# A fused cross attention, differential attention and feed-forward kernel: more of the transposed context from memory for tiles 5 and 6, tile 6's residual kept on chip, W2's scans in the output projection

## The reference

```python
# cross attention, x1 = layernorm(x)
energy = einsum('bcn,bmn->bcm', x1, ctx)          # 64 x 1601 for each batch
attn = softmax(energy, axis=-1)
attn = attn / (1e-9 + attn.sum(axis=1, keepdims=True))
x_r = einsum('bcm,bmn->bcn', attn, ctx)
t = x1 - (einsum('oc,bcn->bon', conv_w, x_r) + conv_b)
t_bn = (t - mean) * rsqrt(var + eps) * gamma + beta   # mean and var over all batches
x = x + x1 + relu(t_bn)
...
# feed-forward: the threshold of W1 and of W2 is 0.05 * max(abs(W))
```

## Time and profile before

| what | value |
|---|---|
| median of three runs | 1365.68 us |
| profiled execution | 1365.15 us |
| its span on the core | 1363.3 us |
| TensorE busy | 1321.5 us, 97% |
| VectorE busy | 867.5 us, 64% |
| ScalarE busy | 486.5 us, 36% |
| moved by DMA | 363.05 MB, mean 266 GB/s |

### The profile page before, as it was taken

How to read it: one execution, slowest core, us unless ns; L and a number is a source line. 1 busy time by engine, 2 the same in 40 slices (tenths; PEclk the granted TensorE clock), 3 DMA queues, 4 the chain that set the end, 5 groups by cost and what they waited for, 6 DMA issues and landing times.

```text
span 1363.3 us, 17544 instructions
## 1 busy us (share of the span) xinstructions
PE 1321.5 (97%) x6738; PEld 642.8 (47%) x6738; DVE 867.5 (64%) x1470; ACT 486.5 (36%) x751; POOL 2.4 (0%) x10
## 2 busy tenths in 40 slices
PE   6999999999999889999999999999999999999995
PEld 4554646444353344444555555445444444444442
DVE  2332424224231379868899986876999997777974
ACT  1111302112020022127777784112555455444432
POOL 0000000000000000000000000000000000000000
PEclk9999999999999989999999999999999999999997
DMA  9999999999999989916656669452477775222264
GB/s 380 419 420 420 420 421 421 422 420 420 406 406 420 412 330 331 325 30 186 173 149 182 170 200 329 148 211 87 168 259 239 231 263 190 77 77 74 78 182 154
DMA packets 142210, 363.05 MB, mean 266 GB/s; under 512 B 63152, under 2 KB 89904, under 8 KB 115760
## 3 DMA queue, kind: packets, MB, share of 16 engines
q1 hardware_dynamic: 138960, 350.39, 70.2%
q10 hardware_dynamic: 3168, 11.54, 2.1%
HBM read 315.22 MB, written 46.66 MB: 265 GB/s over the span
## 4 chain that ended last, share of the span: by engine, by line
PE 79%; issue 14%; DMA 4%; DVE 2%; ACT 0%; DVEq 0%; POOLq 0%; POOL 0%; ACTq 0%
PE ps L1249 14%; PE ps L1133 12%; PE ps L1405 9%; PE ps L1203 8%; PE ps L1316 8%; PE ps L1023 7%; PE ps L1365 6%; PE ps L1061 4%; PE ps L1043 2%; DMA ctxT<-in_ctxT 2%; PE ps L1115 2%; PE ps L1040 1%; PE ps L1269 1%; DMA xo<-in_x 1%; DMA x_t<-in_x 1%
## 5 line engine op out<-in xcount | busy, mean ns | idle before, releaser
L1454 PE MATMUL ps<-t_half,hl 128*128 128x512 f16 x896 | 193.5, 379 | 0.0
L1133 PE MATMUL ps<-ctx_sb,attnT 128*64 128x512 f32 (+1 forms) x832 | 180.3, 593 | 0.0
L757 ACT ACTIVATE stg<-ps 128x512 f32<-128x512 f32 (+1 forms) x66 | 36.3, 552 | 297.5 <-PE ps L1043 169.1
L1454 PEld LDWEIGHTS ps<-t_half,hl 128*128 128x128 f16 x896 | 87.7, 98 | 105.7
L1023 PE MATMUL ps<-ctxT,x1T 128*64 128x512 f32 x512 | 114.9, 596 | 0.4 <-DMA ctxT<-in_ctxT 0.4
L933 ACT ACTIVATE hl<-hb,al 128x512 f16<-128x512 f32 x112 | 79.2, 720 | 97.5 <-PE ps L1454 83.7
L1133 PEld LDWEIGHTS ps<-ctx_sb,attnT 128*64 128x64 f32 (+1 forms) x832 | 59.0, 137 | 115.3 <-issue 107.9
L1972 DVE SCALAR_TENSOR_TENSOR hl<-hb,al,hl 128x512 f16<-128x512 f32 x112 | 81.9, 749 | 48.7 <-ACT hl L933 48.5
L1203 PE MATMUL ps<-wv_sb,x2T 128*128 128x512 f32 x256 | 112.2, 596 | 0.0
L1316 PE MATMUL ps<-wo_sb,oT 128*128 128x512 f32 x256 | 111.6, 593 | 0.3 <-ACT oT L839 0.3
L1527 DVE SCALAR_TENSOR_TENSOR x1s<-ps,sw,x1s 128x512 f32<-128x512 f32 x16 | 12.0, 749 | 133.1 <-PE ps L1133 133.1
(11 more groups left out here) (227 smaller groups left out, 1803.7 us busy)
## 6 DMA issues: line engine op xcount, KB each, us to landing
ctxT<-in_ctxT SPq DMA_DIRECT2D x64, 1024.0 KB, 21.9
ctx_sb<-in_ctx SPq DMA_DIRECT2D x40, 1024.0 KB, 20.1
ctx_sb<-in_ctx SPq DMA_DIRECT2D x8, 4096.0 KB, 27.6
ctx_sb<-in_ctx SPq DMA_DIRECT2D x16, 2048.0 KB, 31.6
w_scan<-in_w1t SPq DMA_DIRECT2D x32, 512.0 KB, 6.3
w_buf<-in_w1t SPq DMA_DIRECT2D x32, 512.0 KB, 3.9
w_scan<-in_w2t SPq DMA_DIRECT2D x32, 512.0 KB, 5.0
w_buf<-in_w2t SPq DMA_DIRECT2D x32, 512.0 KB, 4.7
```

What stands on the lines that cost most here:

```text
L1133: ins = mm(bank(ea + hf)[C * b:C * b + C, :], attnT[0:w, slots[mt], C * b:C * b + C], ctx_sb[0:w, mt, b, hf * BANK:hf * BANK + BANK], star ...
L1454: ins = mm(bank(b), hl[:, r % RING, n, s * P:s * P + P], t_half[:, r % BRING, :], start=(fresh and k == 0 and n == 0), stop=(k == HK - 1 a ...
```

## The change

1. `LOADED` becomes (0, 0, 0, 0, 0, 4, 8, 8): tile 5 has four of its eight chunks of blocks 8 to 11 from memory, tile 6 all eight. Tile 6 then has only the two halves of block 12 left to transpose (`pairs(6)` is of length 2), so the work that was tied to the third and fifth last pair is tied to the first (`max(len - 3, 0)` and `max(len - 5, 0)`).
2. The load of blocks 0 to 3 is split in two halves (group 5, `part`), and the order of SyncE's loads for tiles 5 and 6 is written out.
3. The t of tile 6 is not stored and loaded back: `relu` reads it, as that of tile 7, from `x1s`. `tok` of tiles 2 to 5 is loaded in place of 2 to 6.
4. 32 scans (all of W1) are done beside V, and the 32 of W2 after the last head: 4, then 5 in each tile of the output projection until none is left (28 of them, in six tiles).

```diff
@@ -56,7 +56,7 @@
 U = len(UNITS)
 
 SINGLES = [(mt, half) for mt in range(TM, MT) for half in range(2)]
-LOADED = (0,) * (NT - 2) + (4, NC)
+LOADED = (0,) * (NT - 3) + (4, 8, NC)
 
 
 def pairs(p):
@@ -73,7 +73,7 @@
 
 def slots_of_tile(p):
 
-    ring = [(p, "chunk", c) for c in range(NC)] + [(p, "wide", i) for i in range(min(LOADED[p] // 2, 2))]
+    ring = [(p, "chunk", c) for c in range(NC)] + [(p, "wide", i) for i in range(LOADED[p] // 2 if p < NT - 1 else 2)]
     return ring if p < NT - 1 else ring + [(p, "apart", i) for i in range(2)]
 
 
@@ -88,8 +88,8 @@
 HC = HID // P
 WT = HID * N // P // 1024
 WH = WT // H
-SCANS_V = 40
-V_SCANS = (0, 0, 2, 6, 7, 7, 7, 7, 4)
+SCANS_V = 32
+V_SCANS = (0, 0, 1, 5, 6, 6, 7, 7, 0)
 EPS = 1e-5
 LAMBDA_INIT = 0.8 - 0.6 * math.exp(-0.3 * 12)
 X_SCALE = 512.0
@@ -459,8 +459,14 @@
                 for i in range(2):
                     sp.dma_start(tails[i][:, :, :, :], ctxE_in[i]).then_inc(apart_got, 16)
 
-            def load_N(q, g):
+            def load_N(q, g, part=None):
                 m0, m1 = N_GROUPS[g][0], N_GROUPS[g][-1] + 1
+                if g == 5 and part is None:
+                    load_N(q, g, 0)
+                    load_N(q, g, 1)
+                    return
+                if g == 5:
+                    m0, m1 = 2 * part, 2 * part + 2
                 sp.dma_start(ctx_sb[:, m0:m1, :, :], ctx[q, m0 * P:m1 * P].rearrange("(t p) b n -> p t b n", p=P))\
                   .then_inc(ctx_in[g], 16)
 
@@ -480,10 +486,10 @@
             load_T(1, range(4, 6))
             for p in range(NT - 1):
 
-                def next_N(groups):
+                def next_N(groups, part=None):
                     for g in groups:
                         sp.wait_ge(pv_done, G * p + g + 1)
-                        load_N(p + 1, g)
+                        load_N(p + 1, g, part)
 
                 load_T(p + 1, range(6, 7))
                 if p + 1 < BY_ROW:
@@ -493,6 +499,23 @@
                 else:
                     load_T(p + 1, range(7, NC))
                     load_T(p + 1, range(min(LOADED[p + 1] // 2, 2)), "wide")
+                    if LOADED[p + 1] and p + 1 < NT - 1:
+                        if LOADED[p + 1] == 4:
+                            next_N(range(0, 5))
+                            next_N((5,), 0)
+                            load_T(p + 2, range(0, 4))
+                            next_N((5,), 1)
+                        else:
+                            next_N((4, 0, 1))
+                            load_T(p + 1, range(2, 4), "wide")
+                            next_N((2,))
+                            load_T(p + 2, range(0, 2))
+                            next_N((3,))
+                            load_T(p + 2, range(2, 4))
+                            next_N((5,))
+                        next_N(range(6, G))
+                        load_T(p + 2, range(4, 6))
+                        continue
                     if p + 1 == NT - 1:
                         load_apart()
                         next_N((5, 7, 0, 1, 2, 6, 3, 4))
@@ -501,9 +524,9 @@
                 if p == 0:
                     sp.dma_start(lam_sb[:, 0:4 * D], lambdas.partition_broadcast(P)).then_inc(lam_in, 16)
                 if p + 2 < NT:
-                    load_T(p + 2, range(0, 4 if p < 2 or LOADED[p + 1] else 2))
+                    load_T(p + 2, range(0, 4 if p < 2 else 2))
                 next_N(range(5, 6))
-                if p >= 2 and p + 2 < NT and not LOADED[p + 1]:
+                if p >= 2 and p + 2 < NT:
                     load_T(p + 2, range(2, 4))
                 next_N(range(6, G))
                 if p + 2 < NT:
@@ -517,13 +540,13 @@
                 sp.dma_start(xo[:, t0:t1, :], x_v[t0:t1].rearrange("t p n -> p t n")).then_inc(s, 16)
 
             sp.wait_ge(ctxT_used, len(USES))
-            sp.wait_ge(n_stored, 16 * (NT - 1))
+            sp.wait_ge(n_stored, 16 * (NT - 2))
             load_tok(0, 2)
             sp.wait_ge(pv_done, G * NT - 7)
             load_xo(0, 2, s_in[0])
             sp.wait_ge(pv_done, G * NT - 3)
             sp.dma_start(wv_sb[:, :, :], wv.rearrange("(c p) n -> p c n", p=P)).then_inc(wv_in, 16)
-            load_tok(2, NT - 1)
+            load_tok(2, NT - 2)
             load_xo(2, NT, s_in[1])
             sp.wait_ge(pv_done, G * NT)
 
@@ -546,7 +569,7 @@
                 scan_load(n, w_scan)
                 if n == 8:
                     load_qk(1)
-                if n == 34:
+                if n == 28:
                     sp.wait_ge(xs_ready, 6)
                     load_qk(0)
                 if n == 24:
@@ -746,7 +769,7 @@
             put_x1T(0)
             load_x(1)
             for p in range(NT):
-                if p:
+                if 1 <= p < NT - 1:
                     act.wait_ge(cv_free, 2 * p)
                     act.dma_start(n_dram[p - 1], x1s[:, (p - 1) % 2, :]).then_inc(n_stored, 16)
                 for e, pair in enumerate(pairs(p)):
@@ -757,7 +780,7 @@
                     A(stg[:, e % 4, 0, 0:n], bank(pair_bank(p, e, 0), n), ACT.Copy).then_inc(act_tr_out, 1)
                     if e == (2 if not LOADED[p] else 0) and p + 1 < NT:
                         sqrt(p + 2, slice(0, 1))
-                    if e == 8 and p + 2 < NT:
+                    if e == min(8, len(pairs(p)) - 1) and p + 2 < NT:
                         load_x(p + 2)
                 if p + 1 < NT:
                     put_x1T(p + 1)
@@ -775,7 +798,7 @@
             act.wait_ge(bn_ready, 2)
 
             def relu(t):
-                src = tok[:, t, :] if t < NT - 1 else x1s[:, 1, :]
+                src = tok[:, t, :] if t < NT - 2 else x1s[:, t % 2, :]
                 A(tok[:, t, :], src, ACT.Relu, bias=bnm[:, 7:8], scale=bnm[:, 6:7]).then_inc(relu_done, 1)
 
             def put_v(t, hf):
@@ -1027,7 +1050,7 @@
             def pair_transposes(p, e):
                 kind, a = pairs(p)[e]
                 n = pair_no(p, e)
-                for g in [e // 2] if e % 2 == 0 and p < BY_ROW else range(4) if e == 0 else [4] if e == len(pairs(p)) - 2 else []:
+                for g in [e // 2] if e % 2 == 0 and p < BY_ROW else [4] if e == len(pairs(p)) - 2 else range(4) if e == 0 else []:
                     pe.wait_ge(ctx_in[g], 16 * p + 16)
                 if e == 0 and p:
                     pe.wait_ge(at_out, U * p)
@@ -1128,7 +1151,7 @@
                         w = width(mt)
                         pe.wait_ge(at_out, U * p + 1 + next(u for u, mts in enumerate(units) if mt in mts))
                         g = next(k for k, mts in enumerate(N_GROUPS) if mt in mts)
-                        pe.wait_ge(ctx_in[g], 16 * (p + 1))
+                        pe.wait_ge(ctx_in[g], (32 if g == 5 else 16) * (p + 1))
                         for b in range(2):
                             ins = mm(bank(ea + hf)[C * b:C * b + C, :], attnT[0:w, slots[mt], C * b:C * b + C],
                                      ctx_sb[0:w, mt, b, hf * BANK:hf * BANK + BANK], start=(mt == order[0]), stop=(mt == order[-1]))
@@ -1160,15 +1183,15 @@
                 weigh_ctx(p)
                 if p + 1 < NT and LOADED[p + 1]:
                     chunk_energies(p + 1, range(4, NC))
-                    if p == 5:
-                        loaded_energies(6)
-                        two(pair_transposes, 6, 0)
-                        two(pair_transposes, 6, 2)
-                        two(pair_energies, 6, 0)
-                        later_pairs(6)
+                    loaded_energies(p + 1)
+                    if p + 1 < NT - 1:
+                        two(pair_transposes, p + 1, 0)
+                        if len(pairs(p + 1)) > 2:
+                            two(pair_transposes, p + 1, 2)
+                            two(pair_energies, p + 1, 0)
+                        later_pairs(p + 1)
                     else:
-                        loaded_energies(7)
-                        tail_energies(7)
+                        tail_energies(p + 1)
                 elif p + 1 < NT:
                     chunk_energies(p + 1, range(4, NC - 1))
                     two(pair_transposes, p + 1, 0)
@@ -1550,10 +1573,10 @@
                         V.wait_ge(e_done, first_pair(p) + e - 3)
                     V.wait_ge(dve_tr, pair_no(p, e) + 1)
                     V.tensor_copy(stg[:, e % 4, 1, 0:n], bank(pair_bank(p, e, 1), n)).then_inc(dve_tr_out, 1)
-                    if e == len(pairs(p)) - 3:
+                    if e == max(len(pairs(p)) - 3, 0):
                         V.wait_ge(ctxT_used, used_by(p))
                         own.done(V.tensor_reduce(mx4[:, 0:1], ps[:, ea * BANK:(ea + 2) * BANK], AX.X, ALU.max))
-                    if e == len(pairs(p)) - 5 and p + 1 < NT:
+                    if e == max(len(pairs(p)) - 5, 0) and p + 1 < NT:
                         make_x1(p + 1)
                 if p < NT - 1:
                     V.wait_ge(e_done, first_pair(p + 1) - 2)
@@ -1929,7 +1952,7 @@
                     t_low(4, 0)
```

(2 more changed lines are left out.)

## The result

| what | before | the change |
|---|---|---|
| median (5 runs each) | 1365.95 us (1365.51 to 1367.25) | 1372.90 us (1372.47 to 1373.29) |
| profiled execution | 1365.15 us | 1372.90 us |
| its span | 1363.3 us | 1370.9 us |

The ratio is 1.0049, with an interval of 1.0038 to 1.0060: the change makes the kernel slower, by 6.95 us between the medians and 7.6 between the spans.

A forecast was written before the change was run, and what follows sets the result against it. The prediction took the full DMA queue, through `xo` ahead of V, to bound the stage: 8.7 us of added queue less a 2.0 us gap is +6.7, and 1365.15 + 6.7 gives 1371.8 us, range 1369.5 to 1375.0 (about 0.8).

The forecast's parts named there:

- What bounds the stage: Ahead of V, TensorE and the DMA queue end together; the queue, through the load of `xo`, is on the chain.
- The sum, 1371.8 us: Whole kernel: the profiled 1365.15 us plus 6.7 us, 0.45% above the median; chance 0.72 for 1370 to 1373.5.
- The gap of 2.0 us: DMA queue's idle stretch around 366 to 378 us: the longer queue fills it, taking 2.0 us off the added loads.
- Tile 5, -3.7 us: Tile 5's energies on TensorE: four chunks loaded instead of transposed take 21.7 us instead of 25.4.
- Tile 6, -1.1 us: Tile 6's energies: -3.7 for transposes, -0.6 for a wait gone, +3.2 for waiting on VectorE's row of work.
- Tile 7: Tails land at 438.4 us, TensorE waits 3.5; weighted sum starts 12.5 later at 450.9, ends 473.4, covered by `xo`.
- V to the end: After the stage TensorE runs without waits, so +6.7 us at V's start is +6.7 us at the end.
- The scans, 0 to +0.5: Moving eight scans from beside V to the projection gains nothing; cost taken as none, between 0 and +0.5 us.
- Slack that the rows hide: Rival for the DMA queue: added 3.5 MB could cost nothing and `xo` move with TensorE, 1360.4 us; chance 0.07.
- even: Rival: the queue absorbs two thirds of the 6.7 us, in the gap and TensorE's earlier frees, 1367.4 us; chance 0.07.
- Later still: Rival: TensorE's clock returning late into V, or a late last weighted sum, adds 1 to 4 us: 1374; chance 0.14.
- The rule beside the rows: Price of added DMA bytes: ports' 435 GB/s gives a sum of +6.4 us, HBM share of about 358 gives +8.2.

The follow-up runs named there:

- e048: The change with `LOADED` as before (tiles 5 and 6 at 0 and 4 chunks), its other edits kept: 1365.76 us against 1365.64 for the kernel before.
- b_both_xo: The kernel before, with the first `xo` issued ahead of `tok` and `both(0)` moved behind the last residual: 1366.10 us against 1365.86.
- e448_both_xo: The change with tile 6 at four loaded chunks, the first `xo` issued ahead of `tok`, and `both(0)` behind the last residual: 1364.71 us against 1365.96 before.
- e448: The change with tile 6 at four loaded chunks instead of eight: 1368.05 us against 1365.64 for the kernel before.
- x1_early: The change with tile 7's square root and `make_x1(7)` ahead of tile 6's copies: 1372.59 us, ratio 1.0048 to the kernel before.
- both_late: The change with `both(0)` moved behind `residual(7)` and the batch norm's sum: 1369.50 us, ratio 1.0027 to the kernel before.
- e248_both_xo: The change with `LOADED` (2, 4, 8) for tiles 5 to 7, first `xo` ahead of `tok`, `both(0)` behind the last residual: 1363.49 us against 1365.86 before.
- xo_first: The change with SyncE issuing the first `xo` ahead of `tok` of tiles 0 and 1: 1370.71 us, ratio 1.0034 to the kernel before.
- a_both_xo: The change as it is, with the first `xo` ahead of `tok` and `both(0)` behind the last residual: 1369.89 us, ratio 1.0028 to the kernel before.
- scans40: The change with the scans placed as before, 40 beside V and 4 a tile in the projection: 1373.74 us, ratio 1.0055 to the kernel before.

## Why the prediction was right

- **What bounds the stage.** Right. The chain goes through `xo` before and after, and from e048 to the change each MB ahead of it costs 2.48 us. e048 and b_both_xo show the tie that the prediction read from 471.3 beside 469.2.
- **The sum, 1371.8 us.** Measured 1372.9, the range holds it. The queue's term was +6.7; `xo` landed at 476.5 where 475.9 was forecast, and tile 7's last block at 471.4 against 470.7.
- **The excess of 0.9 us** (7.6 of span against 6.7). 0.7 of it is the later landing of `xo` (+7.37 against +6.7), 0.2 lie between the landing and V (12.5 us instead of 12.3). Tile 5's energies also began 0.8 us late, ahead of anything that the table changes, but such a late start doesn't move the landing: in e448_both_xo they began 1.2 us later than in e448, and `xo` landed 2.5 us earlier, the price of the 1 MB taken from ahead of it.
- **The gap of 2.0 us.** The term that was sized too large. The queue's full bill is +8.7, the landing moved by 7.4, so the gap gave 1.3; in e048 it gave 1.3 too (2.6 less 1.25 for the store), in e448 0.9 (3.74 less 2.87). Its reason was wrong in part as well: the prediction lets the longer queue fill the dip of the earlier trace rows, and e048 has it filled without an added load. The number suffered little, since the change has the split load too. Its sign "420 without a dip" came out at 411 and 406 GB/s from 366 to 378 us, which is (6 x 10 + 6 x 15)/421 = 0.4 us of the queue's time. Why not 421 is open.
- **Tile 5, -3.7 us.** Right: 336.18 - 314.47 = 21.7 us.
- **Tile 6, -1.1 us.** Wrong: 392.11 - 368.81 = 23.3 us instead of 21.7, so +1.6. The term +3.2 for VectorE's row was right (3.05 measured). Missing were 2.1 us of waiting for the loaded chunks, which the playing forward didn't look for (two of them stand in the queue between the blocks of `ctx_sb`), and some 0.7 for the 32 short matmuls after the wait, 1.75 us where they take 1.08. (The prediction's "32 small ones" for block 12's transposes are 16; its time of near 1 us is right, 1.14 by the same 16 before.) Off the path: x1_early took 3 us out of this row and got 0.3.
- **Tile 7.** The tails at 439.06 (438.4 forecast), the wait 3.3 us (3.5), the weighted sum at 453.17 (450.9). The step that failed is "the weighted sum began 12.5 us later": it began 14.1 us later. The 16 matmuls behind the wait took 6.63 us, not the 3.43 of the same number in tile 6, and by luck 1.65 of these 3.2 us came back in `weights_T` (3.14 us instead of 4.79). `xo` covered it, so it cost the change nothing, but the cover was thin: the weighted sum ended at 475.7, 0.9 us ahead of `xo`, where the prediction had 2.5. Once `xo` is out of the way it does: both_late keeps 3.9 us over the kernel before, where the prediction gave TensorE alone +2.1.
- **V to the end.** Right, and to the tenth by luck: 881.8 us both times, where the profiled executions of the other kernels without a new wait inside V have 881.5 to 882.8. The wait on line 1205 grew to 5.4 (some 6 forecast).
- **The scans, 0 to +0.5.** Within what can be told: e048 is 0.1 us from the kernel before with the change's scans in place.
- **The rivals.** "Slack that the rows hide" and "even" fell with e448: 1.5 MB net cost 2.4 us. The price by rows is 3.74 us less the gap, 1.3 by e048, which is the 2.4 measured (2.9 in the landing). "Later still" has its mechanism (the clock, the late weighted sum) but not its price, since `xo` still came last.
- **The rule beside the rows.** Over 3.5 MB added the stretches stayed at 418 and 421 GB/s where the queue was full. The Trainium skill (DMA: Bandwidth & Descriptors, "Where 436 GB/s comes from") gives 435 for the ports and about 358 for a core's share of HBM, and says that for loads from HBM the share binds. The trace agrees with the first as a ceiling, and the share does not bind here: this core, running alone, passes 358 in every one of the first 14 slices. The measured +6.95 lies between the prediction's two sums, +6.4 and +8.2, and alone would not decide. The 4 MB from e048 to the change do: they cost 9.9 us, where an estimate by 435 is 9.6 and by 358 is 11.7. What the share is with other cores at work, no run here shows.

## What to carry to other kernels

Where TensorE is busy for 97% and the DMA engines are full too, look at which of them the end of the stage waits for, and price an exchange of one for the other at the full rate of both: here 1 MB of loads takes 2.5 us of the queue and saves 1.85 us of transposes (3.7 for 2 MB; 1.6 for the 1 MB of e248_both_xo), so the exchange pays only where the queue has room. Where the queue has an idle stretch, see first whether a load that is already there can be split and issued earlier; in e048 the stretch was filled that way, with no load added. Where two resources end together, relieving one brings at most the distance to the next, so move the hand-over (a small job of VectorE that waits for a load) behind the work that doesn't need the load, and only then look for the balance: the two edits of the end gave nothing on the kernel before, and 2.4 us together with a quarter of the change's added loads (1 of 4 MB) and its other edits.

## What the runs showed of the hardware

**A short wait of TensorE costs more than itself.** After 3.3 us of waiting for the tails the granted clock from 440 to 450 us is 0.74 in the change, and 16 matmuls took 6.63 us instead of 3.43: that is the lower of the two levels, 1.2 instead of 2.4 GHz, for nearly all of them. So the wait took 6.5 us of time, not 3.3. The same 16 matmuls took 6.1 to 6.4 us behind waits of 3.3 to 4.0 us in both_late, xo_first and a_both_xo, and 5.35 us behind the shorter ones of x1_early (2.4 us) and scans40 (2.2 us).

**The clock a little later differs between kernels, also where TensorE waited for no tails.** Tile 7's `weights_T`, 26 matmuls behind a wait of 3.4 us for the softmax, took 3.14 us in the change and in e248_both_xo, 4.79 in the kernel before, and 5.9 in e048 and b_both_xo. The stretch 440 to 450 in e248_both_xo:

```profile
440.00:450.00 10.00, 6.87 (x44) 4.27 (x46) 5.19 (x23) 3.21 (x5) 0.00 (x0) 1.00 1.01 419
```

and in the kernel before:

```profile
440.00:450.00 10.00, 6.64 (x58) 5.64 (x54) 5.23 (x20) 3.21 (x5) 0.00 (x0) 0.83 1.01 421
```

What sets it was not tried. It makes up to 2.8 us in a kernel whose stage ends with TensorE, and may be part of the spread from run to run (the kernel before took 1363.71 to 1367.94 us in 31 runs).

**An issue on SyncE's queue can last.** Single loads took 2.1 to 2.9 us to issue in some places (and 2.441 above) and 0.33 in others, with the DMA engines busy in both places (424 and 421 GB/s). The long ones had a landing 24 to 28 us behind the issue, the short one 18, but the rule isn't that simple: `tok` in the change took 0.38 us and landed 28.2 later. The chain of the changed kernel runs through five issues of 2.1 to 6.1 us, from 400.00 to 415.43, and then the tails' landing. Whether they delay the tails, or only show at SyncE that the queue is full, was not tried; counted in MB alone the prediction had the tails at 438.4, and they landed at 439.06.
